# Attention stage of a two-layer kernel: one turned bank per head, two alternating work banks, and another order on three engines

## The reference

```python
    def _L0_xattn_ref(x, latents, mask, g_x, b_x, g_l, b_l, w_q, w_kv, w_out, g_o, b_o):
        ...
        xn = _ln(x, g_x, b_x)
        ln = _ln(latents, g_l, b_l)
        q = ln @ w_q
        kv_in = jnp.concatenate([xn, ln], axis=1)
        k, v = jnp.split(kv_in @ w_kv, 2, axis=-1)
        ...
        q, k, v = (split(q) * scale, split(k), split(v))
        sim = jnp.einsum('bhid,bhjd->bhij', q, k)
        ...
        attn = jax.nn.softmax(sim, axis=-1)
        out = jnp.einsum('bhij,bhjd->bhid', attn, v)
        out = out.transpose(0, 2, 1, 3).reshape(B, Lq, H * DH)
        return _ln(out @ w_out, g_o, b_o)
```

## Time and profile before

| | |
|---|---|
| median of 3 runs | 2255.57 us (2255.49 to 2255.9) |
| span of the profiled execution | 2253.4 us, 2.2 us under the median; what lies around the span isn't in the profile |
| TensorE busy in the span | 2227.8 us (99%) |
| TensorE weight loads | 1877.8 us (83%) |
| VectorE | 1771.8 us (79%) |
| ScalarE | 1284.9 us (57%) |
| GpSimd | 668.4 us (30%) |

### The profile page before, as it was taken

One profiled execution on the slowest core, in us unless ns is written; L12 is line 12 of the kernel. 1 busy time (PEld: TensorE's weight loads), 2 busy tenths in 40 slices (PEclk: granted clock), 3 DMA queues, 4 the chain that ended last, 5 costly groups with the idle time before them and its releaser, 6 DMA issues. The chain is left out here.

```text
span 2253.4 us, 48207 instructions
## 1 busy us (share of the span) xinstructions
PE 2227.8 (99%) x15396; PEld 1877.8 (83%) x15396; DVE 1771.8 (79%) x6078; ACT 1284.9 (57%) x3250; POOL 668.4 (30%) x1162
## 2 busy tenths in 40 slices
PE   8999999999999999999999999999899999999998
PEld 5777777777777777777799999999788888888887
DVE  5888888888888888888775555555599999999997
ACT  6776777677777777776544333433354554555553
POOL 1123233233233232232220000001355555555542
PEclk9999999999999999999999999999999999999999
DMA  6221010010110010110052222222221121222210
GB/s 235 73 95 31 27 40 30 29 39 29 31 38 27 32 39 27 33 32 27 15 155 85 85 72 80 85 66 69 63 60 60 60 62 54 63 64 64 63 43 19
DMA packets 111641, 129.55 MB, mean 57 GB/s; under 512 B 14898, under 2 KB 98089, under 8 KB 111264
## 3 DMA queue, kind: packets, MB, share of 16 engines
q1 hardware_dynamic: 98249, 105.06, 14.4%
q0 software_dynamic: 12288, 21.21, 3.3%
q10 hardware_dynamic: 855, 0.19, 0.0%
HBM read 84.26 MB, written 54.53 MB: 62 GB/s over the span
## 5 line engine op out<-in xcount | busy, mean ns | idle before, releaser
L715 ACT ACTIVATE a_prob<-a_prob,a_nmax 128x376 f32<-128x376 f32 x512 | 307.0, 604 | 3.4 <-DVE a_nmax L861 3.2
L1440 ACT ACTIVATE e_hidden<-e_first,keep_b 128x256 f32<-128x256 f32 x320 | 134.3, 472 | 282.5 <-PE e_first L80 279.5
L1132 PEld LDWEIGHTS a_turned<-keep_ident,a_prob 128*128 128x128 f32 x1518 | 174.2, 139 | 121.3 <-issue 103.6
L861 DVE CUSTOM_DVE_ANT_0 a_prob<-a_score,a_mask_row 128x376 f32<-128x376 f32 x512 | 262.9, 542 | 13.9 <-DVE r_lg L263 6.2
L1132 PE MATMUL a_turned<-keep_ident,a_prob 128*128 128x128 f32 x1518 | 260.5, 280 | 2.2 <-ACT a_probT L723 1.2
L723 ACT ACTIVATE a_probT<-a_turned 128x384 f32<-128x384 f32 x256 | 125.9, 492 | 221.2 <-PE a_turned L1132 216.1
L80 PE MATMUL e_second<-e_w,e_hidden 128*128 128x256 f32 x1920 | 239.6, 284 | 0.0
L80 PEld LDWEIGHTS e_second<-e_w,e_hidden 128*128 128x128 f32 x1920 | 232.6, 192 | 0.0
L177 POOL TENSOR_SCALAR r_var<-r_mv 128x2 f32<-128x2 f32 x64 | 12.3, 192 | 673.1 <-issue 600.0
L873 DVE TENSOR_SCALAR a_prob<-a_prob,a_rden 128x376 f32<-128x376 f32 x512 | 206.9, 431 | 2.2
L880 DVE COPY a_probT<-a_turned 128x384 f32<-128x384 f32 x250 | 139.2, 557 | 82.6 <-PE a_turned L1132 78.4
(11 more groups left out here) (223 smaller groups left out, 5165.3 us busy)
## 6 DMA issues: line engine op xcount, KB each, us to landing
w_in<-W SPq DMA_DIRECT2D x32, 512.0 KB, 4.0
slots<-a_zeros SPq DMA_DIRECT2D x8, 1280.0 KB, 8.9
keep_rows<-slots SPq DMA_DIRECT2D x40, 256.0 KB, 3.9
answers<-e_y SPq DMA_DIRECT2D x40, 256.0 KB, 2.2
a_xn<-x SPq DMA_DIRECT2D x32, 256.0 KB, 2.9
a_xr<-x SPq DMA_DIRECT2D x32, 256.0 KB, 2.9
x<-r_x SPq DMA_DIRECT2D x32, 256.0 KB, 3.2
w_in<-x SPq DMA_DIRECT2D x32, 256.0 KB, 2.7
```

Of the source, the lines that this page charges most:

```text
L715: nc.scalar.activation(prob[:, u % 4, a], prob[:, u % 4, a], ACT.Exp, bias=nmax[:, u % 4, a:a + 1], scale=-1.0, accum_out=den[:, u % 4, a: ...
L861: nc.vector.tensor_tensor_reduce(prob[:, u % 4, a], score[SCORE_AT[u][a]][:, 0:NKV], mask_row[:, p], -1.0, 3.0e38, ALU.add, ALU.min, nmax[ ...
L1132: last = nc.tensor.transpose(turned_keys(b, u, a)[0:hi - lo, j], prob[:, u % 4, a, lo:hi], ident[:])
L1440: nc.scalar.activation(hidden[:, 2 * j + i], first[:, j, i * CH:(i + 1) * CH], ACT.Relu, bias=b1[:, 2 * j + i, bass.ds(e, 1)]).then_inc(re ...
```

## The change

- `turned` becomes two banks, one for each head. `turn_prob(b, u)` now turns both heads in one go, six turns; each head waits for its own `norm_ok` and for its own bank (`prob_ok[a]`).
- The three banks `work[0]`, `work[1]` and `values` become two, `bank_a` (which is `values`, keep_bank in a profile) and `bank_b` (a_work). Every product of the stage outside scores and turns takes one of them, mostly in alternation. The waits in front of the products follow the new neighbours in the bank.
- `times_v(b, p, m)` stands directly behind two `scores` of other groups.
- `output` waits for all four `att_low` before its first product.
- The orders of `step` on TensorE, ScalarE and VectorE are new. GpSimd's and the DMA queue's are as before.
- In the last step 7 and 20 fillers stand around `turn_prob(b, 3)` in place of the table of 46.

```diff
-        turned = pb("a_turned", [P, 512])
-        work = [pb(f"a_work{i}", [P, 512]) for i in range(2)]
+        turned = [pb(f"a_turned{a}", [P, 512]) for a in range(2)]
+        bank_a, bank_b = values, pb("a_work", [P, 512])
...
             def turn_c(b):
                 eng.wait_ge(xh_ok, 3 * (b + 1))
-                at_least(eng, att_lo, KI * (b - 2) + 3)
+                at_least(eng, v_ok, 3 * (b - 1) + 2)
...
             def project_v(b, p, j):
                 if j == 2:
-                    eng.wait_ge(q_hi, 2 * b + 2)
-                    eng.wait_ge(kvin_lo, 2 * (b + 1))
+                    eng.wait_ge(k_hi, KI * b + 2)
...
                 elif j == 1:
                     eng.wait_ge(v_ok, 3 * b + 1)
+                    at_least(eng, att_lo, KI * (b - 1) + 3)
+                elif b == 0:
+                    eng.wait_ge(kvc_ok, KD * 2)
                 else:
-                    eng.wait_ge(k_hi, KI * b + 4)
+                    eng.wait_ge(att_lo, KI * b)
...
-            def turn_prob(b, u, a):
...
-                    at_least(eng, prob_ok[1 - a], NG * b + u + a)
...
+            def turn_prob(b, u):
+
+                for a in range(2):
+                    eng.wait_ge(norm_ok[a], NG * b + u + 1)
+                    at_least(eng, prob_ok[a], NG * b + u)
+                    for j, lo, hi in VALUE_ROWS:
+                        last = nc.tensor.transpose(turned_keys[a][0:hi - lo, j], prob[:, u % 4, a, lo:hi], ident[:])
+                    last.then_inc(turned_ok[a], 1)
...
             def output(b):
...
-                eng.wait_ge(att_lo, KI * b + 3)
+                eng.wait_ge(att_lo, KI * (b + 1))
                 for i in range(QT):
                     for k in range(KI):
-                        if i == 0 and k == KI - 1:
-                            eng.wait_ge(att_lo, KI * (b + 1))
...
+                    times_v(s - 2, p, 0)
+                    if s == B + 1:
+                        eng.wait_ge(y1_ok, QT * (B - 1))
+                        keep_busy(nc, bank_a[:, 0:P], ident[:], ident[:], 7)
+                    turn_prob(s - 2, 3)
```

More of the change, by code:

```diff
@@ L482, in attend @@
         LAST = 3
-        def turned_keys(b, u, a):
-            bank = work[0] if b == B - 1 and u > 1 and a == 1 else turned
-            return bank[:, 0:3 * P].rearrange("p (j q) -> p j q", j=3)
+        turned_keys = [turned[a][:, 0:3 * P].rearrange("p (j q) -> p j q", j=3) for a in range(2)]
         def live(b, last=B):
@@ L693, in k_high @@
                     at_least(eng, score_ok[a], NG * (b - 1))
-                nc.scalar.activation(kT[:, p, m], work[0][:, 0:NKV], ACT.Copy).then_inc(k_hi, 1)
+                nc.scalar.activation(kT[:, p, m], (bank_b if m < 2 else bank_a)[:, 0:NKV], ACT.Copy).then_inc(k_hi, 1)
             def q_high(b, p, i):
@@ L709, in v_out @@
                 nc.scalar.activation(vo[0:rows, p, j].rearrange("p m a d -> p (m a d)"),
-                                     work[0 if j == 0 else 1][0:rows], ACT.Copy).then_inc(v_ok, 1)
+                                     bank_b[0:rows], ACT.Copy).then_inc(v_ok, 1)
             def exps(b, u, a):
@@ L728, in att_high @@
                 at_least(eng, out_ok, b)
-                nc.scalar.activation(att2[:, 0, m], values[:, 0:S], ACT.Copy).then_inc(att_hi, 1)
+                nc.scalar.activation(att2[:, 0, m], (bank_a if m == 1 else bank_b)[:, 0:S], ACT.Copy).then_inc(att_hi, 1)
             def w1_higher(n):
@@ L747, in step @@
                 if live(s - 2):
-                    v_out(s - 2, p, 1)
                     turned_out(s - 2, 1, 0)
+                    exps(s - 2, 4, 1)
                 if live(s - 1):
@@ L762, in step @@
                 if live(s - 2):
-                    att_high(s - 2, 0)
-                    turned_out(s - 2, 3, 0)
-                    exps(s - 2, 6, 1)
+                    turned_out(s - 2, 4, 0)
+                    exps(s - 2, 7, 1)
                 if live(s - 1):
-                    q_high(s - 1, q, 1)
+                    q_high(s - 1, q, 0)
+                    k_high(s - 1, q, 1)
+                if here(s - 3):
+                    x1_standardise(eng, s - 3, q)
+                if live(s - 1):
+                    exps(s - 1, 0, 0)
+                    exps(s - 1, 0, 1)
+                if live(s - 2):
+                    att_high(s - 2, 1)
+                    turned_out(s - 2, 5, 0)
+                if isinstance(s, int) and s == B + 1:
+                    w1_higher(0)
+                    w1_higher(1)
+                if live(s - 1):
+                    exps(s - 1, 1, 0)
+                    v_out(s - 1, q, 2)
+                    exps(s - 1, 1, 1)
+                    k_high(s - 1, q, 2)
+                if live(s - 2):
+                    turned_out(s - 2, 6, 0)
+                if here(s - 3):
+                    router_in(eng, s - 3, bank_b)
                 if live(s):
@@ L956, in step @@
                 if live(s - 2):
-                    over_sum(s - 2, 4)
+                    turned_out(s - 2, 2, 1)
                 if routed(s - 4):
-                    counts_in(eng, s - 4)
+                    counts_in(eng, s - 4, bank_b)
                 if live(s - 3):
@@ L980, in step @@
                     row_max(s - 2, p, 7, 1)
-                    normalise(s - 2, 5, 1)
-                if routed(s - 4):
-                    place(eng, s - 4, p)
+                if here(s - 3):
+                    out_norm(eng, s - 3, q)
                 if live(s - 2):
+                    over_sum(s - 2, 5)
                     normalise(s - 2, 5, 0)
                     turned_out(s - 2, 4, 1)
-                    att_low(s - 2, 1)
+                if here(s - 3):
+                    x1_stat(eng, s - 3, q)
+                if live(s - 2):
+                    normalise(s - 2, 5, 1)
                     over_sum(s - 2, 6)
@@ L1018, in step @@
                     row_max(s - 1, q, 2, 0)
+                    row_max(s - 1, q, 2, 1)
+                    over_sum(s - 1, 0)
                 if live(s - 2):
                     att_low(s - 2, 2)
-                if live(s - 1):
-                    over_sum(s - 1, 1)
-                    row_max(s - 1, q, 2, 1)
-                    row_max(s - 1, q, 3, 0)
+                if here(s - 3):
+                    logits_in(eng, s - 3, bank_a)
                 if live(s - 2):
@@ L1027, in step @@
                 if live(s - 1):
+                    row_max(s - 1, q, 3, 0)
+                    normalise(s - 1, 0, 0)
+                    normalise(s - 1, 0, 1)
                     row_max(s - 1, q, 3, 1)
+                if here(s - 3):
+                    logits_shift(eng, s - 3)
+                if live(s - 1):
+                    over_sum(s - 1, 1)
+                    turned_out(s - 1, 0, 1)
+                    normalise(s - 1, 1, 0)
                     normalise(s - 1, 1, 1)
-                    normalise(s - 1, 1, 0)
+                    row_max(s - 1, q, 4, 0)
                 if here(s - 3):
```

333 lines of the change are left out of this document (138 added, 195 removed).

## The result

The changed kernel takes 2282.57 us (median of 4 runs, 2280.71 to 2283.67) against 2255.74 for the kernel before on the same chip (4 runs, 2255.49 to 2257.49): a ratio of 1.0116, 95% interval 1.0104 to 1.0129. It is slower by 1.2%. The forecast was 2256 us with a range of 2238 to 2272, so it was wrong by 27 us. The profiled execution spans 2280.8 us.

What follows compares the result with a forecast made beforehand. TensorE's own sequence was taken as the bound. Profiled 2253.4 us, plus 5.4 (thirty steps at 34.25 us, 33.41 + 0.84), less 3.1 at the start and 1.4 at the end, plus 2.2 to the median: 2256 us, range 2238 to 2272.

Steps and rivals of the forecast that it cites:

- the end of the stage: Last step of the attention stage, up to the end of the output product: forecast to save 1.4 us (bounds -4 and +2).
- VectorE's way from T7 to PV0: From group 7's turns to the first values product: VectorE needs 15.46 us a step, TensorE 14.62.
- TensorE's prices: Costs of changing between unlike TensorE groups, such as 0.17 us into a half-array group, 0.06 out; -0.66 a step.
- the way from PV0 to T7: From the first values product to group 7's next turns: 18.8 us, in which VectorE doesn't set the pace.
- the start: Start of the attention stage: waits for q, the single turned bank and a normalise all go, -3.1 us (bounds 0 and -4).
- step without waits: One attention step on TensorE without waiting: 33.41 us, which is 0.66 below the old 34.07.
- S directly before PV adds nothing: Scores of two query groups directly followed by a values product on TensorE: no extra cost (bounds 0 and 0.23 us).
- the second rival: The direct join of scores to values product costs 0.17 to 0.23 us each: 2266 to 2270 us, chance 0.14.
- the 0.84 of lateness: TensorE waits 0.84 us a step for VectorE, at the first values product, part of it earlier at project_v(0).
- done some 0.05 to 0.2 us ahead: ScalarE's standardise and two exps between router_in and att_high(2) finish 0.05 to 0.2 us before project_v(1) needs them: no cost.
- the third rival: Two work banks in place of three make TensorE wait for evacuation, 0.3 us a step at project_v(1): 2265 us, chance 0.12.
- the waits of T6 and R for x1_stat: In the last step, group 6's turns and the router's turns wait for x1_stat; with output's wait about +1 us.

Runs made afterwards that it cites:

- e14_best: Changed kernel with eight calls moved on VectorE, GpSimd and ScalarE and the last stage's fillers placed elsewhere: 2243.45 us.
- e10_split: A reordered version of the changed kernel (2264.74 us) with turn_prob 3 and 5 put back between scores and values product: 2281.61 us.
- e13_high2: Changed kernel with one edit, ScalarE's att_high(2) ahead of exps(2,1): 2280.12 us.
- e12_low3: Changed kernel with one edit, VectorE's att_low(3) ahead of over_sum(2), row_max(4,1) and normalise(2,0): 2279.36 us.
- e2_stat: Changed kernel with VectorE's stat moved from ahead of out_stat to ahead of att_low(1), and GpSimd's norm0 behind norm2: 2273.69 us.
- e4d_stat_choose: Changed kernel with the moves of e2_stat, and VectorE's choose moved into the next step behind normalise(2,1): 2266.77 us.
- e7d_low3: e6d_stat_act with VectorE's att_low(3) ahead of over_sum(2), row_max(4,1) and normalise(2,0): 2262.31 us.
- e5_act: Changed kernel with ScalarE's att_high(0) ahead of the two exps of group 6: 2274.06 us.
- e6d_stat_act: Changed kernel with the edits of e2_stat and e5_act together: 2273.88 us.
- e1_tail: Changed kernel with only the last stage's fillers moved: the 20 ahead of group 4's turns removed, 27 put at later waits: 2277.02 us.

## Why the prediction was wrong

By size, four terms of the sum were off: the end of the stage by 9.7 us, VectorE's way from T7 to PV0 by 8.7 (with 2 of TensorE's prices in it), the way from PV0 to T7 by 6 (2 of it prices), and the start by 2.5.

**Right: TensorE's prices.** The forecast's step without waits was 33.41. The groups without waits add up to 33.56, and e14_best has 33.65 with 0.08 of waits. The terms that were short: T7 in front of V 0.61 in place of 0.57, T2 behind the count 0.78 in place of 0.75, and several hundredths elsewhere, 0.15 together (4.5 us in thirty steps).

**Right: S directly before PV adds nothing.** S 1.46 and PV 1.45 in the mean, so the second rival is refuted, and e10_split prices the joins at 0.18 each when they are undone. The Trainium skill (TensorEngine Tiling, Tiling Modes, Key Properties) says that a change of tiling mode drains TensorE; e10_split agrees that a change costs something, with two more such changes a step and 0.39 us more at their places. The direct change from S to PV shows no price of its own: S takes 1.46 ahead of PV, as it does ahead of turns in the earlier trace rows.

**Right in mechanism, off in size: VectorE's way from T7 to PV0.** Forecast 15.46, measured 15.75; of the 0.84 of lateness 0.79 shows where it was said, at V0 (0.71) and PV0 (0.08). The trace splits the 15.75 as the forecast did: from T7 to its evacuation 0.89 (forecast 0.86), VectorE's piece up to counts_in 14.53 (14.3), from there to PV0 0.32 (0.29). 0.11 of the piece is the evacuation of T0, which waits since V1 and with it T0 are late; in e13_high2 that gap is gone and the piece is 14.41. e12_low3 shows that it binds as a way: taking the wait at V0 away brings most of it back at O and PV0. e2_stat shows the other side: making the way to PV0 shorter doesn't help while att_low(3) is late. Single edits brought it to 15.55 at best (e2_stat); only both together (e4d_stat_choose, e7d_low3) shortened it to 15.29 and 15.09. There are two joins with the same lateness on one queue, and the sum in the forecast, which had only one lateness of 0.84, was right to within 0.29: +8.7 us in thirty steps.

**The step of the steady part that failed: "From PV0 to the next T7 ... doesn't set the pace", and ScalarE "done some 0.05 to 0.2 us ahead".** From PV0 to T7 the forecast had 18.79 and the trace has 19.00. 0.13 of it are waits at T6 and R; e2_stat, e5_act and e6d_stat_act each take just these away (18.86 to 18.87), so they come from the chain that begins with counts_in: row_max(6), exps(6), att_high(0), att_low(0), x1_stat, norm2, x1_standardise, att_high(1), and from there through att_low(1), row_max(1) and exps(1) to v_out(2), for which R waits. In e2_stat R starts close behind v_out(2) in 3 steps of 26 only. ScalarE was counted by its own busy work. What was left out is that exps(6) at its head wait for a queue that the same forecast called late. V1's 0.26 lie inside T7 to PV0, where VectorE would be late without most of them too, so that e13_high2 gets back only 0.08 a step. That is why the third rival came out as a mixture: its place was right (V1 waits, behind att_low), and its price of 0.3 isn't added but mostly hidden in VectorE's lateness.

The Trainium skill (Perfetto Trace Analysis, Optimizing Tensor Performance, Matmuls) advises to rotate independent groups over different PSUM banks. The runs agree with it as far as they go: every wait of TensorE in the steps named above, at V1, V0, O, C, R, PV3 and PV0, is for a bank's last reader. They also limit it: e14_best has the same two banks and next to no waits.

**The largest term that failed: the end of the stage, -1.4, measured +8.3.** The forecast named the waits of T6 and R for x1_stat but gave them, together with output's wait, about +1, and took fewer fillers as a saving. The rows have the opposite: the fillers ahead of T4 hold it back, and VectorE's way to x1_stat with it; nothing fills the 3.02 us ahead of T6, which waits behind x1_standardise; and TensorE then works at the clock's lower level up to the end of O. A fall of the clock was no term of the forecast. e1_tail takes 8.2 of the 9.7 us of this error back with another placing and number of fillers alone.

**Failed: the start, -3.1, measured -0.6.** The waits for q and for the turned bank went, as said. The one for a normalise stayed (T2 has 0.98 at 36.30, before 0.97 at 37.48), and three others came: C has 0.58 for v_out at 29.77, K0 0.59 for att_low at 42.70, V1 0.36 for att_low at 57.94. Of these only V1's is a wait of the steady steps too; no experiment was made on them alone, so the cause of this term stays open.

The sum: thirty steps 4.5 (prices), 8.7 (T7 to PV0) less 2 of the prices that lie in it, and 4 (T6 and R) make 15; the end 9.7, the start 2.5. With the forecast's 2254.3 that is 2281, the span after.

## What to carry to other kernels

With fewer banks, look at each product's bank and ask where its last reader stands in its queue, and what that queue waits for ahead of it; a count of the queue's busy time doesn't answer this. When two joins of one queue are equally late, an edit on either shows a part only, and the pair shows what it is worth. Work that looks as if it stood in the way may fill a wait: before moving it, see what the engine would do there instead.
